# An attention and mixture-of-experts layer: tokens routed in three sets instead of two, and scatters that wait for the shared network

## The reference, cut to what matters

```python
x = _layernorm(x + attention(x))              # 8 heads of 64, causal, gated
logits = x @ Wg                               # 2048 x 16
_, topi = top_k(logits, 2)
gates = softmax(where(mask_of(topi), logits, -inf))
for e in range(16):
    h = silu(x @ W1[e] + b1[e]) * (x @ W11[e] + b11[e])      # 128 -> 256
    y = y + (h @ W2[e] + b2[e]) * gates[:, e, None]
z = silu(x @ Ws1 + bs1) * (x @ Ws11 + bs11) @ Ws2 + bs2       # 128 -> 512 -> 128
out = _layernorm(x + y + z)
```

## Time and profile before

| | us |
|---|---|
| median of 3 runs | 677.01 (676.71 to 678.45) |
| the profiled execution's own time | 678.42 |
| its span, first to last instruction | 676.66 |
| busy PE, DVE, ACT, POOL | 627.8, 457.1, 387.5, 176.1 |
| from the start to the first product of the shared network | 491.5 |
| from there to the first expert product | 74.8 |
| from there to the end | 110.4 |

### The profile page before, as it was taken

The page is one execution under the profiler, slowest core; times in us unless marked ns, Lnnn a source line. Parts: engine busy times, 40 slices in busy tenths (PEclk is TensorE's granted clock), DMA queues, the critical chain, the costliest instruction groups (busy, mean ns, idle before and its releaser), DMA issues.

```text
span 676.7 us, 14851 instructions
## 1 busy us (share of the span) xinstructions
PE 627.8 (93%) x5286; PEld 505.6 (75%) x5286; DVE 457.1 (68%) x1493; ACT 387.5 (57%) x821; POOL 176.1 (26%) x302
## 2 busy tenths in 40 slices
PE   7999999999999999999999999999994969888875
PEld 5788888778888877888877788888742639787862
DVE  5977767678776767877675887776773344666634
ACT  6765566676556667655666765555541113666643
POOL 5111101231110122111012211101355722666650
PEclk8999999999999999999999999999997979999998
DMA  6499961189990119995011200000393102222215
GB/s 153 110 169 162 153 103 32 33 150 165 163 121 2 32 32 65 4 5 2 2 32 32 64 1 2 2 1 2 128 268 45 45 19 61 74 73 75 64 49 173
DMA packets 112920, 48.55 MB, mean 72 GB/s; under 512 B 53712, under 2 KB 106192, under 8 KB 112848
## 3 DMA queue, kind: packets, MB, share of 16 engines
q1 hardware_dynamic: 109456, 42.20, 44.3%
q0 software_dynamic: 2560, 5.28, 2.3%
q10 hardware_dynamic: 832, 0.14, 0.1%
HBM read 14.78 MB, written 24.43 MB: 58 GB/s over the span
## 4 chain that ended last, share of the span: by engine, by line
PE 80%; DVE 7%; ACT 4%; issue 4%; another core or an unknown queue 2%; DMA 1%; DVEq 0%; POOL 0%; SPq 0%; ACTq 0%; POOLq 0%
PE ps_o L1301 18%; PE ps_t L1163 18%; PE ps_s L1267 10%; PE ps_s L1269 9%; PE ps_s L1435 6%; PE ps_o L1423 3%; PE ps_s L1174 3%; PE ps_o L1163 2%; PE ps_o L1313 2%; PE ps_s L1345 2%; PE ps_s L1171 2%; PE ps_t L1359 2%; DVE q_hl L818 1%; DVE w_now L1114 1%
## 5 line engine op out<-in xcount | busy, mean ns | idle before, releaser
L1163 PE MATMUL ps_t<-ident,probs 128*128 128x128 f32 x1104 | 173.3, 273 | 5.3 <-ACT probs L640 2.1
L1163 PEld LDWEIGHTS ps_t<-ident,probs 128*128 128x128 f32 x1104 | 136.0, 141 | 44.4 <-issue 8.5
L676 ACT ACTIVATE probs<-probs,nmax 128x128 f32<-128x128 f32 (+15 forms) x128 | 153.4, 1199 | 22.9 <-DVE nmax L974 15.9
L983 DVE COPY probsT<-ps_t 128x512 f32<-128x512 f32 (+3 forms) x160 | 91.1, 569 | 100.6 <-PE ps_t L1163 99.3
L687 ACT ACTIVATE probsT<-ps_t 128x512 f32<-128x512 f32 (+3 forms) x160 | 89.4, 558 | 95.4 <-PE ps_t L1163 94.2
L1267 PE MATMUL ps_s<-k_h,q_hl 128*128 128x512 f32 (+3 forms) x320 | 141.0, 444 | 0.4 <-DVE q_hl L818 0.4
L1301 PE MATMUL ps_o<-probsT,v_sb 128*64 128x128 f32 x2176 | 140.0, 277 | 0.1
L548 POOL TENSOR_TENSOR rden<-rsum,minus_one 128x2 f32<-128x2 f32 x64 | 44.3, 693 | 348.8 <-ACT probs L676 337.6
L969 DVE TENSOR_SCALAR_CACHE_REDUCE probs<-ps_s 128x512 f32<-128x512 f32 x192 | 127.6, 685 | 0.3 <-issue 0.3
L1301 PEld LDWEIGHTS ps_o<-probsT,v_sb 128*64 128x64 f32 x2176 | 116.8, 137 | 14.5 <-issue 12.5
L1269 PE MATMUL ps_s<-k_l,q_hl 128*128 128x512 f32 (+3 forms) x320 | 116.9, 366 | 0.0
(11 more groups left out here) (172 smaller groups left out, 754.9 us busy)
## 6 DMA issues: line engine op xcount, KB each, us to landing
x_sorted<-zeros SPq DMA_DIRECT2D x68, 258.0 KB, 9.5
k_h<-k_h SPq DMA_DIRECT2D x32, 128.0 KB, 2.3
k_l<-k_l SPq DMA_DIRECT2D x32, 128.0 KB, 2.3
w_all<-in_L_ffn_W SPq DMA_DIRECT2D x2, 2048.0 KB
xg<-x_sorted SPq DMA_DIRECT2D x48, 65.0 KB, 1.8
act_s<-y_rows SPq DMA_DIRECT2D x3, 512.0 KB, 5.8
x_acc<-in_L_attn_tokens SPq DMA_DIRECT2D x4, 256.0 KB, 4.6
y_rows<-y_sb,row_all POOLq DMA_INDIRECT x48
```

Source lines behind the costliest of these rows:

```text
L676: nc.scalar.activation(probs[s % 2][h][:, 0:w], probs[s % 2][h][:, 0:w], ACT.Exp, bias=nmax[:, row], scale=-1.0, accum_out=rsum[:, row]).t ...
L983: nc.vector.tensor_copy(probsT[s % 2][h][:, c * BT:c * BT + w // P, :].rearrange("p n i -> p (n i)"), ps_t[1][:, 0:w]).then_inc(moved1, 1)
L1163: return nc.tensor.transpose(dst, src, ident[:, :])
```

## The change

Three sets instead of two: `SETS` is now n0 alone (tiles 12 to 15), n1 alone (8 to 11), and n3 with n2 (0 to 7). The first set is routed inside the last pair of heads. Its turning, logits and counts are three PE units (`route`) that use banks of the score ring, so `freed` now counts three more and SP's load of the experts' weights waits for the last of them. Its gates are taken with Exp (the table that attention uses) and a reciprocal on DVE instead of Tanh. POOL takes `row_scale(0)` three tiles earlier, makes the second copy of the set's rows itself, and issues the set's eight scatters around `row_scale(2)` and `row_scale(3)`, before the end of the attention's sums is waited for. Every tile of the second and third set waits for one more product of the shared network (`act_done`) before its two scatters. Three steps of the table of slots are moved to smaller n. Tiles that the first set needs get memory of their own.

```diff
-    SETS = (range(n1 * BT, (n0 + 1) * BT), range(n3 * BT, (n2 + 1) * BT))
+    SETS = (range(n0 * BT, (n0 + 1) * BT), range(n1 * BT, (n1 + 1) * BT), range(n3 * BT, (n2 + 1) * BT))
+    ROUTE_FILLS = 3
+    EARLY_TILES = BT // 2
...
+    s13, s14, s15 = unit("scores", NT - 3, 1, 1, 2 * P), unit("scores", NT - 2, 0, 0, 4 * P), unit("scores", NT - 2, 1, 0, 4 * P)
     PE_UNITS = [pair_units(False, {}),
-                ending(pair_units(True, {}),
-                       [t14a, wo12, pv13, t14b, t15a, wo13, t15b, pv14, pv15, unit("turn_x", c=n0), wo14,
-                        unit("turn_x", c=n1), wo15])]
+                between(ending(pair_units(True, {}),
+                               [t14a, wo12, route_counts, pv13, t14b, t15a, wo13, t15b, pv14, pv15, wo14,
+                                unit("turn_x", c=n1), wo15]),
+                        [(s13, route_x), (s14, route_logits)])]
...
     DVE_UNITS = [pair_units(False, DVE_LAG, True),
-                 ending(ahead(pair_units(True, DVE_LAG, True), unit("times_wo", 10), unit("stats", c=n0)),
-                        [wo12, unit("stats", c=n1), sc13, t14b, unit("norm", c=n0), pv14, wo13, t15a, t15b, pv15,
-                         unit("norm", c=n1), sc14, sc15, wo14, unit("stats", c=n2), wo15, unit("stats", c=n3)])]
+                 between(ending(pair_units(True, DVE_LAG, True),
+                                [wo12, unit("stats", c=n1), route_counts, sc13, t14b, unit("slots", c=n0), pv14, wo13,
+                                 t15a, t15b, pv15, unit("norm", c=n1), sc14, sc15, wo14, unit("stats", c=n2), wo15,
+                                 unit("stats", c=n3)]),
+                         [(unit("times_wo", 9), unit("stats", c=n0)), (unit("scores", NT - 3, 0, 1, 2 * P), unit("norm", c=n0)),
+                          (s13, route_x), (s14, route_logits), (s15, unit("choice", c=n0))])]
...
-            sp.wait_ge(freed, ONE + KQ_FILLS + (PAIRS - 1) * FREED + GROUPS)
+            sp.wait_ge(freed, ONE + KQ_FILLS + (PAIRS - 1) * FREED + GROUPS + ROUTE_FILLS)
             sp.dma_start(w_all[:, :, 0:H], W1.rearrange("e d h -> d e h")).then_inc(moe_in, 16)
...
-                    if p == PAIRS - 1 and s == NT - 1:
+                    if p == PAIRS - 1 and s == summed[n0] + 2:
                         row_scale(0)
+                    if p == PAIRS - 1 and s == summed[n0] + 4:
+                        pool.wait_ge(x1_ready, BT)
+                        nc.gpsimd.tensor_copy(rows1_n0[:, :, 0:D], rows0[:, n0 * BT:(n0 + 1) * BT, 0:D]).then_inc(rows_early, 1)
...
             row_scale(1)
+            pool.wait_ge(zfill, 16 * (groups + E + 1))
...
+            pool.wait_ge(gates_ready, TOPK)
+            pool.wait_ge(slots_ready, 1)
+            for t in SETS[0][:EARLY_TILES]:
+                scatter(t)
             row_scale(2)
+            row_scale(3)
+            for t in SETS[0][EARLY_TILES:]:
+                scatter(t)
             pool.wait_ge(acc_done, ONE + PAIRS * NT)
...
+            products = 1
+            for i in (1, 2):
+                pool.wait_ge(rows_ready, 1 if i == 1 else 3)
                 pool.wait_ge(gates_ready, TOPK * (i + 1))
                 pool.wait_ge(slots_ready, i + 1)
-                for t in tiles:
-                    for k in range(TOPK):
-                        nc.gpsimd.indirect_dma_start(
-                            out=x_sorted, out_offset=bass.IndirectOffsetOnAxis(ap=slot[:, k, t:t + 1], axis=0),
-                            in_=rows[k][:, t, :], in_offset=None).then_inc(scattered, 16)
+                for t in SETS[i]:
+
+                    products += 1
+                    pool.wait_ge(act_done, products)
+                    scatter(t)
...
             act.preload_act_table(ACT.Silu)
-            rows_twice(n0)
             rows_twice(n1)
...
+                def route(k, n):
+
+                    bank, cols = ps_s[n % RING], in_set(0)
+                    dve.wait_ge(fill, p * FILLS + (PROJECTIONS + n + 1))
+                    if k == 0:
+                        nc.vector.tensor_copy(x_turned_of(n0), bank[:, :]).then_inc(freed, 1)
+                    elif k == 1:
+                        dve.wait_ge(route_consts, 10)
+                        nc.vector.tensor_copy(logits[:, cols, :].rearrange("p n e -> p (n e)"),
+                                              bank[:, 0:BT * E]).then_inc(freed, 1)
+                        dve.wait_ge(freed, p * FREED + (KQ_FILLS + n + 1 + ONE))
+                        largest_logits(0)
+                    else:
+                        totals(0, bank[:, P:P + BT * E])
+                        ranks(0, bank[:, 0:BT * E]).then_inc(freed, 1)
...
                 elif n == 9:
-                    gates(1)
+                    tiles_of_experts()
                 elif n == 10:
-                    tiles_of_experts()
+                    gates((2,))
+                    experts_of_slots()
+                elif n == 11:
+                    rows_of_slots()
                 elif n == 12:
                     shared_add(1)
-                elif n == 13:
-                    experts_of_slots()
-                elif n == 14:
-                    rows_of_slots()
```

More of the change, by code:

```diff
@@ L131, in ahead, with between @@
         return units[:at] + [x] + units[at:]
+    def between(units, pairs):
+        for after, x in pairs:
+            units = ahead(units, after, x)
+        return units
     START = [("project", w, 0, c, 0) for w, c in ((K, 0), (Q, 0), (K, 1), (Q, 1), (V, 0), (K, 2), (Q, 2), (V, 1),
@@ L239, in attention_moe_layer, with rows, x_turned_of @@
         gatedT = sb("gatedT", [P, NT // GT8, P], f32, moe)
[L240 to L250, removed]
+        xT = sb("xT", [P, N - BANK], f32, moe)
+        rows1 = sb("rows1", [P, NT - BT, D + 2], f32, moe)
+        def rows(k, tiles):
+            if k == 0:
+                return rows0[:, tiles, :]
+            if tiles.start >= n0 * BT:
+                return rows1_n0[:, tiles.start - n0 * BT:tiles.stop - n0 * BT, :]
+            return rows1[:, tiles, :]
+        def x_turned_of(c):
+            return xT_n0[:, :] if c == n0 else xT[:, c * BANK:(c + 1) * BANK]
         cnt_i = sb("cnt_i", [P, E], i32, moe)
@@ L566, in _, with number_rows, scatter @@
                     nc.gpsimd.tensor_tensor(b2_pad[:, :, :], b2_pad[:, :, :], bs2_pad[:, :, :], ALU.add).then_inc(b2_summed, 1)
+            def number_rows(k, tiles):
+                nc.gpsimd.iota(rows(k, tiles)[:, :, D + 1].bitcast(i32), pattern=[[TOPK * P, len(range(NT)[tiles])]],
+                               base=TOPK * P * tiles.start + k, channel_multiplier=TOPK).then_inc(numbers_set, 1)
+            def scatter(t):
+                for k in range(TOPK):
+                    nc.gpsimd.indirect_dma_start(
+                        out=x_sorted, out_offset=bass.IndirectOffsetOnAxis(ap=slot[:, k, t:t + 1], axis=0),
+                        in_=rows(k, slice(t, t + 1))[:, 0, :], in_offset=None).then_inc(scattered, 16)
@@ L907, in largest_logits, with take_logits, choose @@
                                         ALU.subtract).then_inc(gate_diff, 1)
+            def take_logits(i):
+                cols = in_set(i)
+                dve.wait_ge(lg_psum, 1 if i == 1 else 3)
+                link(nc.vector.tensor_copy(logits[:, cols, :].rearrange("p n e -> p (n e)"),
+                                           logit_bank((n1, n2)[i - 1])[:, cols.start * E:cols.stop * E]))
+            def choose(i):
+                cols, tiles = in_set(i), len(SETS[i])
                 for t in SETS[i]:
@@ new lines, in slots, with place, gates @@
+                nc.vector.tensor_copy(slot[:, :, cols], slot_f[:, :, cols]).then_inc(slots_ready, 1)
+            def place(i):
+                bank, width = count_bank(i), len(SETS[i]) * E
+                totals(i, bank[:, 3 * P:3 * P + width])
+                link(ranks(i, bank[:, 2 * P:2 * P + width]))
+                slots(i)
+            def gates(sets):
+                for i in sets:
+                    cols = in_set(i)
+                    dve.wait_ge(gates_ready, TOPK * (i + 1))
+                    for k in range(TOPK):
+                        ins = nc.vector.tensor_tensor(gated[:, k, cols], hot[:, k, cols],
+                                                      rows(k, cols)[:, :, D].unsqueeze(2).to_broadcast([P, len(SETS[i]), E]),
+                                                      ALU.mult)
@@ L1017, in pair @@
                         norm(stage, c)
+                    elif stage == "route":
+                        route(s, fill_of[x])
+                    elif stage == "choice":
+                        choose(0)
+                    elif stage == "slots":
+                        dve.wait_ge(freed, p * FREED + (KQ_FILLS + fill_of[route_counts] + 1 + ONE))
+                        slots(0)
             for p in range(PAIRS - 1):
@@ L1333, in pair @@
                         norm(stage, c)
+                    elif stage == "route":
```

(3 more changed lines are left out.)

202 lines of the change are left out of this document (119 added, 83 removed).

## The result

| | us |
|---|---|
| before, median of 6 runs (the 3 shown and 3 more beside the new kernel) | 678.74 (676.71 to 679.11) |
| after, median of 6 runs | 673.77 (671.94 to 674.71) |
| ratio | 0.993, 95% interval 0.9915 to 0.9945 |
| span of the profiled executions | 676.7 before, 673.0 after |
| forecast | 666.7, range 656 to 680 |

The sign and the place were right, the size was not: 5.0 us came of the 10.3 forecast, and both holes are still there. The forecast was worked out on the first 3 runs of the kernel before (677.01); on the median of all 6 it would be 668.4, so that doesn't explain the miss.

What follows compares the result with a forecast made beforehand. Slow signals between engines during POOL's back-to-back scatters after attention were taken to cost two holes; +0.5 - 5.4 - 5.4 = -10.3 us on the median of 677.01 gave 666.7 us, range 656.0 to 680.0.

Steps and rivals of the forecast that it cites:

- both holes: Two stretches after attention where signals between engines turn slow during back-to-back POOL scatters; 9.4 and 10.9 us lost.
- The size of the holes before: Kernel before, shared network's stage: first hole costs 9.4 us up to `slot`, second 10.9 us up to the last `shared_down`.
- Routing inside the last pair: End of attention and tail: moved DVE work makes PE lose 1.0, tail +1.0, smaller set -1.5; sum +0.5 us (-1 to +3).
- POOL and SP, nothing: POOL's row copy and early scatters, and SP's later weights and biases, stay hidden or have slack: no cost.
- the slower case: Rival: signals slow already in the tail, from 498.8 to 514.3, giving 681.5 us; chance 0.16.
- First hole, 4.0 taken as left: Second set's scatters: signals good from 514.3, loss 0 to 5.8, 4.0 taken; saved 9.4 - 4.0 = 5.4 us.
- The rule itself: Stretch after attention: each hole closes 4.0 us after the last scatter of its run started (544.80 to 548.83).
- Second hole, 5.5 taken as left: Third set: six or seven tiles go before waits bind; loss 4.5 to 7.0, 5.5 taken; saved 10.9 - 5.5 = 5.4 us.
- ACT's hole 4 to 8 us: Sign that the forecast is right: ACT's hole before its thirteenth step lasts 4 to 8 us instead of 14.2.
- The holes didn't vanish: Rival on the shared network's stage: split runs of scatters never reach the slow point, both holes vanish, 657.2 us; chance 0.28.
- the change does what it says: Against the rival that waits never bind and holes depend on something else, or gains are given back: 677.5 us; chance 0.12.
- The hole didn't open in the tail: Rival: counting starts with the first early scatter at 489.3; `slot` comes 6.1 us later, nothing saved; 681.5 us, chance 0.16.

Runs made afterwards that it cites:

- The last two runs: The changed kernel and the kernel before, profiled on a chip without holes: 642.77 against 642.24, ratio 1.0026; one more execution of the kernel before took 641.62.
- the waits alone: The kernel before with a wait on act_done for each tile of its two sets, nothing routed early: 669.14, ratio 0.9873 to the kernel before.
- the kernel with higher counts: The changed kernel with its third set waiting for 9 to 13 products, on chips without holes: 645.58 to 646.71, ratios 1.0043 to 1.0074 to the kernel before.

## Why the prediction was right or wrong

The last two runs give what was missing for an account: both kernels with and without holes. Read from the four timelines, with the differences worked out (us):

| | before, holes | before, none | lost | after, holes | after, none | lost |
|---|---|---|---|---|---|---|
| first product of the network | 491.50 | 491.16 | | 493.57 | 493.87 | |
| from there to `slot` of the last set | 33.3 | 23.2 | 10.1 | 29.4 | 21.7 | 7.7 |
| from there to the last `shared_down` | 40.1 | 29.1 | 11.0 | 37.5 | 28.7 | 8.8 |

The columns "lost" take the chip without holes for what the other would do without them. That is an inference; for it speaks that attention ends at the same point on both, within 0.4 us.

**The size of the holes before** was right: 10.1 and 11.0 against 9.4 and 10.9.

**Routing inside the last pair, +0.5 (-1 to +3):** right. The first product comes 2.1 us later (2.7 without holes), with PE waiting 1.4 us for DVE where it waited 0.4 before, close to the 1.0 that I took; this row of PE's waits from 460 to 494 in the kernel after shows it (total, times, longest):

```profile
PE ps_o L1416 <- DVE outT L1086: 1.4, 2, 1.1
```

By the first `act_s` it is 1.2 (496.37 against 495.15), and by the last `shared_down` without holes 0.85 (544.34 against 543.49).

**POOL and SP, nothing:** right. The early scatters take 0.96 us beside a busy DVE, the first 1.34; those at 499.97 and 501.23 took 0.96 while DVE wrote its norms at 499.87 and 501.60. The Trainium skill, page SBUF — State Buffer, has in the section "SBUF: two separate sides" that some fp32 copies of VectorE lock such a DMA's descriptors out, and in "A bandwidth-pool intuition that's wrong" 3100 ns for one that takes 620 alone. These rows don't show it, and the slower case for which the prediction cited it did not come.

**First hole, 4.0 taken as left: the step that failed, first half.** 7.7 was left, so 2.4 was saved and not 5.4. DVE could have had its logits copy at 508.0 (508.32 on the chip without holes, less 0.3 for the later start there) and had it at 514.62, so 6.6 went: above the bound of 5.8 and far above the 4.0 that I chose, although the hole opens early in the run. 0.5 of this is that I took 508.5 for the undisturbed copy. That the end was foreseen (514.3) is in part luck: the last of the 12 scatters started 1.3 us later than forecast, and DVE went 3.0 us after it and not 4.0.

The rule itself, that signals are good from 4.0 us after the last scatter, came from the second hole alone. The first hole of the kernel before doesn't obey it. Its last scatter started at 518.51, so the rule says 522.5, and these two went on before that (ACT and DVE):

```profile
513.71 0.69 ACT L736 ACTIVATE sil_s<-ps_s,bs_col 128x512 f32<-128x512 f32 x1 [4.02 <-issue]
520.03 0.42 DVE L917 TENSOR_TENSOR hot<-ie,idxf 128x256 f32<-128x256 f32 x1 [3.11 <-issue]
```

In the kernel after, ACT went on 0.8 us after the last scatter's start and DVE 3.0. In these two holes hand-overs are late, each by its own amount; they are not stopped until a common end.

And behind the hole PE ran at its lower clock: 2.07 and 1.91 us for two pairs of products that take 1.13 and 1.02 without the hole. From the logits copy to `slot` it takes 8.4 us and 7.3 without a hole (508.32 to 515.59), so this is the other 1.1. I had priced the clock for the second hole only.

**Second hole, 5.5 taken as left: the same step, second half.** 8.8 was left, so 2.2 was saved and not 5.4. I said six tiles or seven and took a value between them. The case of seven gives ACT's thirteenth step at slots + 21.2; it came at 522.97 + 21.3 = 544.28. The closeness is luck again: the run started 1.0 us after the slots and not 0.8, its 14 scatters took 16.9 us and not 16.4, and ACT went 3.4 us after the last start and not 4.0. It could not have been six. The seventh tile waits for 12 products, and in the traces with holes the network makes 12 before the hole bites, as the earlier trace rows show for ACT's steps; only the eighth tile waits for the thirteenth. So the waits were one tile from doing nothing.

The rest is 2.4 us where I took 0.8 for the clock and what follows: from ACT's thirteenth step to its sixteenth it takes 7.7 us (544.28 to 551.98) and 5.3 without a hole (530.57 to 535.84), at a granted clock of 0.67 over 544 to 551.8. My own rows had this price: six products in 5.2 us where the usual pace gives 2.6 are 2.5 us, not the 1.3 that I called clock.

The sum by these: +0.2 for the routing (a start 2.1 later, less the 1.5 and 0.4 by which the table's two stretches are shorter without holes), -2.4, -2.2, together -4.4 at the last `shared_down` (560.49 against 564.94). The expert stage, 110.4 before, takes 111.2, for which I have no cause, so that 3.7 is left in the spans; the medians, of executions of their own, give 5.0.

**Slips in the prediction's own numbers.** The sign "ACT's hole 4 to 8 us" contradicts the 5.5 us taken as left: ACT waits 5.5 us there without any hole, so that loss of 3.7 to 6.2 gives 9 to 12, and 10.8 was measured. The bounds of the two holes allow 5.0 us less and not 4.0, so the forecast's own range begins at 660; at its other end, 673, the measured 673.77 lies just outside.

**The rivals.** The holes didn't vanish. The waits did bind, if once, and taking them out cost 0.5%, so the change did what it says. The hole didn't open in the tail: the hand-overs up to 504 are prompt. On a chip without holes the change is slower by 0.26%, less than the 0.3% that the prediction counts as a change, and not by that rival's way: the two timelines there differ by 0.85 us at the last `shared_down`, the price of the routing, and by 0.35 in the expert stage (94.90 against 94.55).

**What stays open.** What fills up or slows down in a hole; what differs between a chip at 678 and one at 642 (or between their surroundings or times), and whether it is the same thing that makes the experts' stage 16 us longer there; whether SP's bias DMAs add to the first hole (the second opens with no other queue at work, so they aren't needed for one); at what distance between 1.26 and 1.57 us the holes go; and whether the changed kernel lags behind the waits alone (0.993 against 0.987) by the low counts of its waits or by the early routing, as the kernel with higher counts met no chip with holes.

## What to carry to other kernels

A wait paces an engine only if its count is one that the other side hasn't reached when the trouble starts: read from the trace which count that is, and set the wait there. Idle time on every engine at once with no data behind it, beside a run of back-to-back indirect DMAs, is worth one cheap experiment, a short pause after each; here it took out most of it, 15.8 us together with a change that alone took 5. Don't price such a hole by the time at which it ends: its cost also holds the clock behind it, here 1.1 and 2.4 us. And such a gain belongs to the chip on which it was measured: measure on several, since the same kind of pause, applied to all 32 scatters, cost 11 to 12 us where there was no hole.

## What the runs showed that I had not expected

- One and the same program takes 678 us on one chip and 642 on three others, each steady over the runs it had. By the table above, 21.1 of the difference is holes in the shared network's stage and 15.8 the stage of the experts (110.4 against 94.6); attention takes the same (first product at 491.5 and 491.2).
- There 48 scatters of the expert stage leave POOL little idle time, where the earlier trace rows have 35.8 us (group of POOL, kernel before, 545 to 640 on the chip without holes):

```profile
L601 POOL DMA_INDIRECT y_rows<-y_sb,row_all x48 | 49.3, 1027 | 13.2 <-POOL row_all L592 9.2 <-ACT y_sb L763 2.5 <-issue 1.5
```

- The expert stage of the kernel before on the chip with holes has short waits of the same kind. These are PE's and ACT's, from 566 on (total, times, longest); on the chip without holes neither group shows such a wait:

```profile
PE ps_o L1423 <- issue: 4.7, 11, 0.5
ACT y_sb L763 <- remote: 5.5, 10, 0.6
```

- On the chip with holes, 0.31 us more between two scatters leave 2.2 us of the first hole's 7.7 and 0.8 of the second's 8.8 (`slot` at 517.63, 23.9 after the first product, and the last `shared_down` 29.5 after that).
